# A three-part model on one core: distances of two or more steps in the pipeline of its attention stage, with two bias additions moved off TensorE

## The reference

```python
h = tok_ref(x, ...)                         # 2 layers, 192 wide, banded attention
h = h + attn_ref(_layernorm(h), ind, ...)   # two attention blocks over 128 induced rows
h = h + ffn_ref(_layernorm(h), ...)         # 32 experts, gated in two levels
```

```python
def _mab(q, k, v, p):
    x = q + _mha(_ln(q, g1, b1), _ln(k, g1, b1), _ln(v, g1, b1), in_w, in_b, out_w, out_b)
    h = _ln(x, g2, b2)
    ff = gelu(h @ l1w.T + l1b) @ l2w.T + l2b
    return x + ff
h = _mab(ind_b, x, x, p1)     # 128 queries `ind`, 512 keys: the 128 induced rows
return _mab(x, h, h, p2)      # 512 queries, 128 keys
```

## Time and profile before

| | us |
|---|---|
| median of 3 runs (2573.77 to 2579.31) | 2574.18 |
| the profiled execution, own time | 2564.87 |
| its span | 2563.0 |
| TensorE busy in the span | 2097.3 (82%) |
| VectorE, ScalarE, GpSimd busy | 1300.9, 1125.2, 756.2 |

### The profile page before, as it was taken

The page is one execution under the profiler, slowest core; times in us unless marked ns, Lnnn a source line. Parts: engine busy times, 40 slices in busy tenths (PEclk is TensorE's granted clock), DMA queues, the critical chain, the costliest instruction groups (busy, mean ns, idle before and its releaser), DMA issues. The chain is left out here.

```text
span 2563.0 us, 44046 instructions
## 1 busy us (share of the span) xinstructions
PE 2097.3 (82%) x14745; PEld 1487.9 (58%) x14745; DVE 1300.9 (51%) x4329; ACT 1125.2 (44%) x2396; POOL 756.2 (30%) x950
## 2 busy tenths in 40 slices
PE   5799999999999999999953567778776449999944
PEld 4466666666666666666642345545544239999931
DVE  2466555666555666555623345565444313333358
ACT  2466666665665666665610233333332113333322
POOL 0021212221212221212221012243444525555543
PEclk7799999999999999999975678776766569999965
DMA  3732233342234332233002322223121176777632
GB/s 99 123 66 49 38 41 63 63 63 46 37 45 85 63 63 44 35 50 63 2 2 76 70 51 50 61 69 72 44 52 40 55 247 209 235 230 225 188 98 90
DMA packets 119393, 211.48 MB, mean 83 GB/s; under 512 B 23236, under 2 KB 52038, under 8 KB 118520
## 3 DMA queue, kind: packets, MB, share of 16 engines
q1 hardware_dynamic: 108024, 189.29, 32.5%
q0 software_dynamic: 10176, 17.09, 2.1%
q10 hardware_dynamic: 976, 2.30, 0.3%
HBM read 149.82 MB, written 66.82 MB: 85 GB/s over the span
## 5 line engine op out<-in xcount | busy, mean ns | idle before, releaser
L675 ACT ACTIVATE tower_prob<-tower_prob,tower_negmax 128x386 f32<-128x386 f32 (+1 forms) x768 | 390.4, 556 | 303.2 <-DVE tower_negmax L882 302.5
L882 DVE CUSTOM_DVE_ANT_0 tower_prob<-tower_sbank,tower_band 128x386 f32<-128x386 f32 (+1 forms) x768 | 346.4, 489 | 142.4 <-PE tower_sbank L449 137.1
L487 PEld LDWEIGHTS tower_tbank<-tower_ident,tower_prob 128*128 128x128 f32 x1920 | 227.8, 143 | 129.5 <-issue 81.7
L487 PE MATMUL tower_tbank<-tower_ident,tower_prob 128*128 128x128 f32 x1920 | 284.4, 279 | 22.0 <-DVE tower_probT L907 20.4
L731 ACT ACTIVATE tower_probT<-tower_tbank 128x384 f32<-128x384 f32 (+1 forms) x576 | 227.6, 430 | 127.4 <-PE tower_tbank L487 124.8
L2000 POOL DMA_INDIRECT scratch_yt<-experts_y,experts_rows x190 | 185.8, 978 | 204.1 <-DVE experts_y L2151 171.7
L426 PE MATMUL tower_dbank<-tower_oxT,tower_w 96*128 96x512 f32 x384 | 191.4, 624 | 14.9 <-ACT tower_oxT L720 14.9
L2059 PE MATMUL experts_ybank<-experts_w,experts_hid 128*128 128x128 f32 x1520 | 186.8, 277 | 0.0
L2047 PE MATMUL experts_hbank<-experts_zT,experts_w 128*128 128x256 f32 x760 | 184.2, 386 | 1.0 <-issue 1.0
L449 PE MATMUL tower_sbank<-tower_k_st,tower_q_st 49*128 49x386 f32 (+1 forms) x768 | 161.1, 414 | 26.0 <-POOL tower_k_st L631 14.6
L2059 PEld LDWEIGHTS experts_ybank<-experts_w,experts_hid 128*128 128x128 f32 x1520 | 178.9, 193 | 0.1
(11 more groups left out here) (318 smaller groups left out, 3453.4 us busy)
## 6 DMA issues: line engine op xcount, KB each, us to landing
experts_w<-ew SPq DMA_DIRECT2D x95, 578.0 KB, 3.9
scratch_qk<-tower_qk SPq DMA_DIRECT2D x64, 384.0 KB, 4.8
tower_q_st<-scratch_qk SPq DMA_DIRECT2D x96, 192.0 KB, 7.9
tower_k_st<-scratch_qk SPq DMA_DIRECT2D x96, 192.0 KB, 10.9
experts_rows<-scratch_zs SPq DMA_DIRECT2D x95, 132.0 KB
scratch_kq<-induce_kq SPq DMA_DIRECT2D x8, 1024.0 KB, 4.3
experts_res<-scratch_yt SPq DMA_DIRECT2D x8, 1024.0 KB, 5.5
induce_k_st<-scratch_kq SPq DMA_DIRECT2D x48, 128.0 KB, 4.2
```

The lines of the kernel that those rows point to most:

```text
L487: mm = pe.transpose(bank[:, jb * P:jb * P + P], prob[:, hg % PR, at + jb * P:at + jb * P + P], ident[:, :])
L675: act.activation(prob[:, hg % PR, 0:width(i)], prob[:, hg % PR, 0:width(i)], ACT.Exp, bias=negmax[:, hg % PR:hg % PR + 1], scale=-1.0).the ...
L882: scores.copied(dve.tensor_tensor_reduce(prob[:, hg % PR, 0:width(i)], bank[:, 0:width(i)], band[:, BAND_AT[i]:BAND_AT[i] + width(i)], sca ...
```

## The change

The table of step numbers is rewritten so that two or more steps lie between a piece and its user. A sequence now takes 158 steps where it took 109, and the pipeline runs from step -23 to 246 where it ran from -15 to 205. The period stays 16. Stores of keys go out a step later than the keys (`A_STORE`, `K2_STORE`), the stores of the results at 118. Two steps of the gate and the copy of `z` get numbers of their own.

The bias matmuls go. The biases of the projection `out_b` and of `l2_b` are added by GpSimd, in advance, to the residual: `y1b` is `y1` with the bias of the first down projection, `x2` gets the bias of the second projection, `y2b` that of the second down projection. `x2`, the output `h` standardised, is made just before it is needed (78) instead of beside `x3`, and so has one buffer where it had five. The output `h` is thus normalised at two times, and its moments are kept in a slot for each of its now seven buffers (`slot_of`). Three buffers for `v2`. In the one step with the last GELUs ScalarE does the exponentials after them.

```diff
-        A_STAT, A_NORM, A_X, A_H, A_MOM, A_X3, A_X2 = -15, -13, -12, -11, -10, -8, -7
-        A_U, A_K, A_V, A_STACK = -7, -6, -5, -4
-        S1, M1, T1, V1 = (0, 2, 4, 6), 7, (9, 11, 13, 15), (13, 17)
...
-        S2, M2, T2, V2 = (40, 42, 44, 46), 47, (49, 51, 53, 55), (53, 57)
...
-        NH, NX = 5, 5
+        A_STAT, A_NORM, A_X, A_H, A_MOM, A_X3 = -23, -21, -19, -17, -15, -13
+        A_U, A_K, A_V, A_STORE, A_STACK = -11, -9, -8, -8, -6
+        S1, M1, T1, V1 = (0, 2, 4, 6), 8, (13, 15, 17, 19), (17, 21)
...
+        S2, M2, T2, V2 = (56, 58, 60, 62), 64, (69, 71, 73, 75), (73, 77)
...
+        NH, NV2 = 7, 3
...
+        def slot_of(k, m):
+            return HEAD + m % NH if k == HEAD else k
...
-            def by_rows(key, lhs, rhs, n=NT, bias=None):
+            def by_rows(key, lhs, rhs, n=NT):
                 bank = dense.claim(pe, key)
                 for t in range(n):
-                    mm = pe.matmul(bank[:, t * E:t * E + E], lhs[:, t * P:t * P + P], rhs, start=True,
-                                   stop=bias is None)
-                    if bias is not None:
-                        mm = pe.matmul(bank[:, t * E:t * E + E], onesr[0:1, :], bias, start=False, stop=True)
+                    mm = pe.matmul(bank[:, t * E:t * E + E], lhs[:, t * P:t * P + P], rhs, start=True, stop=True)
...
                         for c in range(IF):
-                            pe.matmul(out, hid2[:, c, t * P:t * P + P], l2[:, 1, c, :], start=(c == 0), stop=False)
-                        mm = pe.matmul(out, onesr[0:1, :], erows[0:1, 1, BL2, :], start=False, stop=True)
+                            mm = pe.matmul(out, hid2[:, c, t * P:t * P + P], l2[:, 1, c, :],
+                                           start=(c == 0), stop=(c == IF - 1))
...
-                    if p == M2:
+                    if p == M2 + 1:
                         lower(1, m, q2_st[j], low2)
...
-                    if p == Y2_NORM:
-                        pool.wait_ge(normed, norm_order[ATT2, m])
+                    if p == Y1 + 1:
...
+                        pool.tensor_tensor(y1b[:, :], y1[:, 0, :], erows[:, 0, BL2, :], ALU.add).then_inc(y1b_ready, 1)
+                    if p == X2_BIAS:
+                        pool.wait_ge(x2_ready, m + 1)
+                        pool.tensor_tensor(x2[:, :, :], x2[:, :, :],
+                                           erows[:, 1, BOUT:BOUT + 1, :].broadcast_to([P, NT, E]), ALU.add)\
+                            .then_inc(x2b_ready, 1)
+                    if p == Y2_SUM:
...
+                        ch.mark(pool.tensor_tensor(y2b[:, :, :], y2[:, :, :], h[m % NH][:, :, :], ALU.add))
+                        ch.after()
+                        pool.tensor_tensor(y2b[:, :, :], y2b[:, :, :],
+                                           erows[:, 1, BL2:BL2 + 1, :].broadcast_to([P, NT, E]), ALU.add)\
+                            .then_inc(y2b_ready, 1)
...
-                for m, p in items(g):
-                    exponentials(m, p)
+                if all(p != UP2[1] for m, p in items(g)):
+                    for m, p in items(g):
+                        exponentials(m, p)
                 for m, p in items(g):
                     pieces(m, p)
+                if any(p == UP2[1] for m, p in items(g)):
+                    for m, p in items(g):
+                        exponentials(m, p)
...
-                if p == A_X2:
-                    normalise(HEAD, m, x2[m % NX], h[m % NH], x2_ready)
+                if p == X2:
+                    normalise(HEAD, m, x2, h[m % NH], x2_ready)
...
                     if m:
                         dense.take(dve, ("x5T", m - 1))
+                        dve.wait_ge(base_ready, m)
                     normalise(FF2, m, x5, h2, x5_ready)
```

92 lines of the change are left out of this document (53 added, 39 removed).

## The result

The changed kernel takes 2446.28 us (median of 4 runs, 2445.05 to 2451.94), the kernel before 2573.97 us beside it: ratio 0.9511, 95% interval 0.9482 to 0.9540. It is 128 us faster. By the ratio, on the median of 2574.18 that the prediction started from, it is 2448.3, just on that end.

The account below looks back on a forecast made before the run. Stage `induce` was taken as bound by dependences between in-order engines, no engine being full. The terms -36 + 3 - 80 + 33 gave -80 us, from a median of 2574.2 to 2494 us, range 2448 to 2565.

Parts of the forecast that it names:

- Bias matmuls, -36: Stage `induce`: 144 bias instructions leave TensorE's queue, taken as wholly on the path, -36 us; nearer -18 if hidden by VectorE.
- Additions on GpSimd, +3: Bias additions moved to GpSimd: 24 additions can each hold up VectorE by 0.9 us, at most 22 us; taken as 3.
- Waits removed, -80: Two steps between maker and user in `induce` remove TensorE's listed waits, sum 86.7 us; taken as -80, bounds -40 and -105.
- the longer pipeline, +33: 49 more steps, 3.06 periods, in `induce` leave thin periods with idle time: between 0 and 57 us, taken as +33.
- The clock, 0: The forecast sum had no clock term: TensorE's remaining 430 us of work in `induce` kept the same granted clock.
- a rival of 38 us: Denser windows in `induce` hold the high clock, another -38 us, 2456; chance 0.20, shared with cheaper ends.
- The end of the stage, 0: No term for GpSimd's final scatters in `induce`; scatters, 1.0 us each, were considered only as standing behind the additions with the roots.
- The slower case: In `induce` each added step costs as now: +85 us, to 2659, or milder +21, to 2595; chance 0.12.
- VectorE becomes the bound: In `induce` only half the waits go because VectorE limits: -40 us, 2534; chance 0.22.
- four groups of waits gone: Sign: TensorE's waits for maxima, r1n, choice and low rows in `induce` gone except in the last sequence.
- TensorE's waits go over to VectorE's tiles: Sign that the forecast is wrong: TensorE's waits in `induce` shift to tiles made by VectorE; no size given.
- At the same clock: Sign: TensorE's busy time in `induce` down by about 41 us with the granted clock unchanged.

Follow-up runs that it names:

- depth16: Against the changed kernel, everything from the second attention's stacks on moved 16 steps later, pipeline one period longer; ratio 0.9591 to the kernel before.
- after_again: The changed kernel run once more unaltered, as a control; ratio 0.9503 to the kernel before.
- spacing_only: The changed kernel's table of steps and buffers, but bias matmuls kept on TensorE and no bias additions on GpSimd; ratio 0.9685 to the kernel before.

## Why the prediction was right in part, point by point

- **Bias matmuls, -36.** Right, and some 5 us too small. Alone they give -41.5 us, in the spaced kernel -43.4 (616.0 to the mean of 572.6), where they are listed with 41.3 and 37.9 us.
- **Additions on GpSimd, +3.** Near enough for the stage, where no cost shows. The busy time of VectorE grows by 13.6 us through them, under the bound of 22, and idle time of TensorE doesn't move.
- **Waits removed, -80, and the longer pipeline, +33: together -47 of idle time.** Measured to the last cast -49.8. Right as a sum; the parts can only be estimated. By depth16's price the pipeline's idle part is 40, so the waits gave about 90 (both rough), in spite of the wait for `yn`, which grew by 32 us and which no part of the prediction foresaw. I had counted the distance in steps and not asked what stands ahead in the same step.
- **The clock, 0.** This is the term that was wrong. The forecast had TensorE's remaining work at the same clock ("busy 466 - 36 = 430"), and kept the other way for a rival of 38 us with a chance of 0.20. It measured -36.4 in the first profiles and -36.6 between the means. The forecast and that rival are not alternatives: one is a sum of work and waits, the other what a denser schedule does to the duration of all work. It should have stood in the sum, since the earlier trace rows already had 0.73 in a dense window and 0.53 to 0.63 in thin ones and the forecast itself made every window denser. (A tenth of 430 would be 43; the rival took 38. And "0.53 to 0.73" left out windows with 0.80 and 0.83.) With -36 in it the sum is -116, against -118.7 measured, but that closeness is in part luck. To the last cast the means differ by -127.9: beside the forecast -80 stand 36.6 for the clock, 5 for the bias matmuls, 3 for the additions and 3 for idle time. The end of the stage then gives some 10 back.
- **The end of the stage, 0.** GpSimd's queue of scatters gives back some 10 us (40.2 us from the last cast to the next stage's first tile, 30.5 before). The prediction looked at the scatters only as something ahead of the roots.
- **Rivals.** The slower case needed 2.4 us a step; depth16 shows 1.5. The time of "VectorE becomes the bound" (2534) did not come, and no full window is filled by it (37.1 busy of 51.3). But its mechanism is there in part: of 186.8 us of listed waits 148.7 are for VectorE's tiles, where they were 134.7 of 239.8, and the choice's wait moved to another tile when its step was moved. What was named as signs came out: full windows 51 us (50 to 58), no rows with erows on TensorE, four groups of waits gone. The choice's wait was named as one that goes, and stayed at 25.4 us in five waits. "TensorE's waits go over to VectorE's tiles" was named as a sign of being wrong; it came, and still the time fell by more than forecast. "At the same clock" and "41 us" for the busy time failed, and they point at the term.

## What to carry to other kernels

In a stage that is bound by dependences, price the clock together with the waits: idle time that goes makes the rest of TensorE's work shorter (here 36 us beside 50), and depth that is added probably makes it longer (12 us in one run). A table of steps says how far a maker and its user are apart, but whether the distance is kept is decided by what stands ahead of the maker in the same step on its engine: look for pieces of two sequences with equal step modulo the period, above all behind an instruction that waits. And when all work moves earlier, look at the engine that drains the queue at the end.

## What the runs showed of the hardware

- The 16 DMAs of pad rows stand in SyncE's queue for 20.4 us in the first profile of the changed kernel and for 39.8 in after_again. In the profiles in which they are slow (34 to 42 us) the next stage starts 43 to 51 us behind the last cast, in the others with this table or one near it 39.5 to 40.5. It goes with the chip: all slow profiles come from two chips, and the fast ones whose chip is on record from two others. The cause isn't known.
- TensorE can be busy in 49.3 of 50 us at a granted clock of 0.66 (spacing_only). Whether the bias matmuls, whose weights have one row, count for less than others there was not tried.
- A switch of ScalarE's function table costs 1.28 us and no more here: the load starts 0.02 us behind the instruction before it, and the exponential 1.29 us behind the load's start.
- Indirect DMAs of 128 rows follow each other in GpSimd's queue at 1.26 us from start to start when nothing stands between them (0.96 us listed), sixteen for a sequence.
